# A graph kernel on one core: gather b is issued only when gather b-2 has landed

## What is computed

```python
def _rgcn_conv(x, W, Wroot, b, src, dst, etype):
    xs = x[src]
    seg = dst * R + etype
    sums = segment_sum(xs, seg, N * R)
    cnt = segment_sum(ones, seg, N * R)
    mean = (sums / maximum(cnt, 1.0)[:, None]).reshape(N, R, -1)
    return x @ Wroot + b + einsum('nrd,rde->ne', mean, W)

h = relu(_rgcn_conv(layernorm(x), W1, Wroot1, b1, ...))
x = x + _rgcn_conv(h, W2, Wroot2, b2, ...)
x = x + ffn(layernorm(x))      # top 2 of 8 experts, 256 -> 1024 (gelu) -> 256
```

## Time and profile before

| | us |
|---|---|
| median of 3 runs without the profiler | 2936.58 |
| lowest and highest of them | 2933.07, 2938.32 |
| span of the profiled execution, first to last instruction | 3487.9 |

### The profile page before, as it was taken

One profiled execution on the slowest core, in us unless ns is written; L12 is line 12 of the kernel. 1 busy time (PEld: TensorE's weight loads), 2 busy tenths in 40 slices (PEclk: granted clock), 3 DMA queues, 4 the chain that ended last, 5 costly groups with the idle time before them and its releaser, 6 DMA issues.

```text
span 3487.9 us, 82172 instructions
## 1 busy us (share of the span) xinstructions
PE 2472.0 (71%) x19212; PEld 1832.7 (53%) x19213; DVE 1780.8 (51%) x4984; ACT 1225.2 (35%) x2344; POOL 1862.5 (53%) x1980
## 2 busy tenths in 40 slices
PE   1346787678687786346776587687877428999999
PEld 0113565356365564114564365465656327888887
DVE  7324455345355454124454354354545338787777
ACT  5202343134243342012343143152432126555554
POOL 1666566655655554666556656655563543333333
PEclk9557999589799898557998798798997559999999
DMA  6223323233332232223333333333335234322222
GB/s 216 80 83 112 88 87 91 85 87 89 87 88 87 86 89 64 86 84 97 98 104 97 94 100 99 94 105 95 101 100 163 102 115 132 96 73 71 71 70 59
DMA packets 165489, 333.24 MB, mean 96 GB/s; under 512 B 36078, under 2 KB 102346, under 8 KB 165288
## 3 DMA queue, kind: packets, MB, share of 16 engines
q0 software_dynamic: 91632, 247.48, 24.1%
q1 hardware_dynamic: 39912, 41.03, 4.0%
q10 hardware_dynamic: 33872, 43.92, 3.9%
HBM read 285.39 MB, written 49.07 MB: 96 GB/s over the span
## 4 chain that ended last, share of the span: by engine, by line
PE 44%; issue 22%; DVE 10%; another core or an unknown queue 9%; DVEq 7%; SPq 2%; ACT 2%; DMA 1%; ACTq 0%; POOLq 0%; POOL 0%
PE more_banks L1408 13%; PE sum_banks L1384 9%; PE sum_banks L1385 7%; PE more_banks L1535 4%; PE sum_banks L1535 3%; PE more_banks L1400 3%; PE sum_banks L1545 3%; DVEq L1044 3%; DVEq L1041 2%; DVE sels L1044 2%; DVEq L1027 1%; DVE stage L1079 1%; DVE sels L1036 1%; PE sum_banks L1426 1%
## 5 line engine op out<-in xcount | busy, mean ns | idle before, releaser
L509 POOL DMA_INDIRECT ring<-table,tabs x1584 | 1526.9, 964 | 1046.4 <-SPq L399 670.0
L1384 PE MATMUL sum_banks<-ring,sels 128*128 x2348 | 726.6, 311 | 630.1 <-issue 420.1
L1408 PE MATMUL more_banks<-weights,stage 128*128 128x256 f16 x5292 | 919.1, 290 | 22.0 <-issue 21.4
L1385 PE MATMUL sum_banks<-ring,sels 128*128 x2348 | 732.2, 313 | 41.5 <-issue 38.7
L1384 PEld LDWEIGHTS sum_banks<-ring,sels 128*128 128x128 f16 (+1 forms) x2348 | 242.4, 103 | 928.2 <-issue 896.9
L683 ACT ACTIVATE stage<-sum_banks,inv 128x256 f16<-128x256 f32 x784 | 328.1, 473 | 789.5 <-issue 384.9
L1408 PEld LDWEIGHTS more_banks<-weights,stage 128*128 128x128 f16 x5292 | 531.1, 104 | 135.3 <-issue 37.1
L1036 DVE SCALAR_TENSOR_TENSOR sels<-lane,win_off,tabs 128x256 f16<-128x256 f16 x792 | 349.4, 482 | 422.1 <-remote 181.9
L654 ACT ACTIVATE stage<-more_banks 128x1024 f16<-128x1024 f16 x392 | 402.0, 1026 | 419.1 <-remote 405.6
L1044 DVE TENSOR_SCALAR sels<-lane,win_off,tabs 128x128 f16 x780 | 260.6, 334 | 495.8 <-issue 339.6
L1079 DVE SCALAR_TENSOR_TENSOR stage<-sum_banks,inv,stage 128x256 f16<-128x256 f32 x784 | 347.0, 479 | 57.2 <-issue 40.2
(11 more groups left out here) (319 smaller groups left out, 2407.5 us busy)
## 6 DMA issues: line engine op xcount, KB each, us to landing
ring<-table,tabs POOLq DMA_INDIRECT x1584
weights<-L_ffn_W ACTq DMA_DIRECT2D x96, 178.5 KB
stage<-L_ffn_W ACTq DMA_DIRECT2D x16, 1024.0 KB, 5.0
edge_work<-lot_in SPq DMA_DIRECT2D x54, 260.0 KB
table<-edge_work ACTq DMA_DIRECT2D x49, 128.0 KB
lot_in<-sels SPq DMA_DIRECT2D x8, 260.0 KB
weights<-L_gnn_W SPq DMA_DIRECT2D x2, 1024.0 KB, 8.3
weights<-L_gnn_W ACTq DMA_DIRECT2D x2, 1024.0 KB
```

What stands on the lines that cost most here:

```text
L509: pool.indirect_dma_start(ring_rows[:, b % RING, 0:2 * D], None, tables[layer], bass.IndirectOffsetOnAxis(row_tab[:, b:b + 1], 0)).then_in ...
L1384: pe.matmul(to[:, 0:D + 1], hot, ring_row[:, ds(at + D, D + 1)], start=first, stop=last, skip_group_check=True)
L1385: return pe.matmul(to[:, 0:D], hot, ring_row[:, ds(at, D)], start=False, stop=last, skip_group_check=True)
L1408: return [pe.matmul(ps_out[par], rows[:, xp * KD + k, :], w16[:, wp, k, r * D:(r + 1) * D], start=part == PART_ORDER[0] and n == 0, stop=p ...
```

## The change

POOL gets one more wait before each gather from the third of a layer on: for the semaphore that the DMA of gather b-2 raises, at the value that says that all of it has landed. It is the same condition on which SP's `landed` waits. The slot wait stays, ahead of it.

```diff
     RING = 16
     AHEAD = RING // 2
+    BEHIND = 2
...
                 for b in range(GATHERS):
                     if b >= RING:
                         pool.wait_ge(slots_free[layer], b - RING + 1)
+                    if b >= BEHIND:
+                        s = (b - BEHIND) % RING
+                        pool.wait_ge(gathered[s], (b - BEHIND) // RING * 16 + 16 * (USES[s] * layer + 1))
                     pool.indirect_dma_start(ring_rows[:, b % RING, 0:2 * D], None, tables[layer],
                                             bass.IndirectOffsetOnAxis(row_tab[:, b:b + 1], 0)).then_inc(gathered[b % RING], 16)
```

## The result

| | before | changed |
|---|---|---|
| median us (4 runs each) | 2937.45 | 3744.24 |
| lowest and highest | 2933.07, 2940.33 | 3739.47, 3747.62 |
| profiled span | 3487.9 | 3736.6 |

The ratio is 1.2749, with a 95% interval of 1.2731 to 1.2767: 807 us slower. The direction and the bound were as forecast, the amount was not: it came to twice the 404 us, outside the range.

What follows compares the result with a forecast made beforehand. POOL's gather rate was taken to bound the graph layers: two gathers take 2.78 + 0.26 us, 1.52 us each; 1582 x 1.52 plus 965.9 us outside, less corrections of 20, 4.3 and 6 us, gives 3340 us, range 3120 to 3450 us.

Steps and rivals of the forecast that it cites:

- the 404 us: Whole kernel: the forecast slowdown, 13.7%, to 3340 us; 68% for 3250 to 3430 us.
- The reading of the bound: Graph layers: the profile's extra 551 us are recording pauses; timed, POOL's gather rate is the bound, 1.246 us per interval.
- the 965.9: Time outside the 1582 gather intervals, in us: 84.3 before the first, 850.1 from the last's start, 31.5 between layers.
- The landing: Graph layers: from a gather's start on POOL to its landing, taken as 2.78 us, with 2.9 us the other end.
- The second wait: POOL from the 17th gather on: likely an instruction for one of two waits, costed at nothing, up to 0.1 us a pair.
- 0.26: POOL's wake, in us, from the release of a wait to the gather's start; bounds 0.2 and 0.3 us.
- my corrections: Taken off the sum: 20 us of backlog at layer ends, 4.3 us at the ring's start, 6 us for the count.
- Rival (a), the slack takes it: Graph layers: 670.0 us of slot waits absorb the longer intervals, about 2937 us, no change; 4%.
- Rival (b), a shorter landing: Gathers land sooner than traced: 0.5 us less gives 2945 us (5%), half of that 3135 us (11%).
- Rival (c): Graph layers: fewer gathers in flight leave POOL's issue undisturbed, 24 us won, 2913 us; 1%.
- Rival (d), late landings: Graph layers: long landings no longer absorbed, 1.60 us an interval, 3467 us; 11%.
- L399's waits: POOL's 574 waits for a free ring slot before gathers, 670.0 us in the profile; forecast to fall by more than half.

Runs made afterwards that it cites:

- The second profile of before: The unchanged kernel before, profiled once more with no edit: 2934.0 us in its one timed run, profiled span 2931.9 us.
- the swapped one: The changed kernel with its two waits in the other order, landing of gather b-2 first, then the free slot: 3360.5 us, ratio 1.146.

## Why the prediction failed, step by step

*The reading of the bound held.* That the 551 us were no part of the timed kernel, that it is bound by POOL's gathers, and that the full cost of an interval would show in the time, all rested on an inference. The second profile of before and the run with less TensorE work bear it out. So do four kernels (the changed one, the swapped one and the two with one gather in flight): with intervals from 1.56 to 3.53 us, what lies outside the intervals stays at 892 to 894 us in their traces, so that all of an interval's growth is in the time. The counting was less good: not all of the pauses lay in the layers, 68 us of the 965.9 were pauses too (965.9 - 897.6), and the interval of the timed kernel before was 1.286 us and not 1.246.

*The landing held.* 2.78 us was taken; the changed kernel's chain shows 2.74, 2.76 and, now and then, more. From a gather's start to SP's mark of its landing the median is 2.77 us and the mean 2.88.

*The second wait is the step that failed.* The prediction costed it "at nothing", with "up to 0.1 us a pair" as its end. It was some 0.48 us a pair (0.74 us in place of 0.26). With the order turned round the changed kernel loses 384 of its 807 us, and 384 is nearly all of the 404 us by which the forecast was short. The 20 us that are left between 3360 and the forecast are two smaller errors against each other: an interval of 1.56 and not 1.52 us (63 us more, 20 of them at the 14 gathers above; late landings can explain the rest), and 42 us too much outside the intervals after my corrections (935.9 against some 894).

The reason for the mistake is in how were read. There the semaphore instruction is followed by a gather 0.31 us behind the last, so it looked free. But it had been over before POOL got to it. It said nothing of an instruction whose wait ends last. The same stage of the kernel before has that case too, and I should have taken it for the upper end: VectorE's two rows end at 3101.67 us, and POOL, whose semaphore instruction (L550) waits for them, starts its transfer 0.98 us later.

```profile
3100.80 0.87 DVE L1305 SCALAR_TENSOR_TENSOR edge_work<-edge_work,lot_w 128x256 f32<-128x256 f32 x2
...
3102.65 1.02 POOL L552 DMA_INDIRECT out<-edge_work,lot_ids  x1 [5.92 <-DVE edge_work L1305]
```

With it in place of 0.26 a pair could have taken up to 2.78 + 0.98 = 3.76 us, 1.88 each, and the range would have reached 935.9 + 1582 x 1.88 = 3910 us. The question that I didn't ask was which of the two waits stands on the gather and which ahead of it.

*Rival (a), the slack takes it,* fell with the pauses. *Rival (b), a shorter landing,* too: the landing is the same in profiles without pauses. The fit of the Trainium skill ("DMA: Bandwidth & Descriptors", Anatomy of one DMA, SWDGE path), which gives an estimate of 2.3 us for such a transfer, isn't borne out here; the traces have 2.7 to 2.8 us from POOL's start to the semaphore. *Rival (c)* had no part: POOL's mean is 962 ns. *Rival (d), late landings,* is real and small: in the run with three in flight they cost 34 us.

*What the profile should have shown.* Starts forecast as 1.25 and then 1.8 us apart came 1.25 and 2.25 us apart. That L399's waits would fall by more than half was wrong in name: the profile's rule puts 976 waits down to its successor, L400. The span was foretold as 3600 to 3800 us and is 3736.6, for another reason than the one given, since no gather caught up in pauses.

## What to carry to other kernels

When a wait is added to an instruction that already has one, ask which of them stays on the instruction and which becomes an instruction ahead of it: the one that ends last should be on the instruction itself, here a matter of swapping two lines and 384 us. A limit of n DMAs in flight makes each take (landing + restart)/n, and is free once that is clearly under the issue time; here 2 is far too few, 3 still costs 1.9%, 8 nothing (4 to 7 were not run). And where a profiled span is much longer than the timed runs, find the stretch before believing any wait in it, or take the profile again.

## What was not expected of the hardware

A gather whose own wait ends last starts 0.24 to 0.3 us after its release. Behind a separate semaphore instruction it starts 0.71 to 0.74 us after that has passed. I take the difference, some 0.48 us, for the time in which POOL makes the gather's instruction ready, which would be over already when the wait is on the gather itself; the runs show its size and that it is hidden behind the gather ahead when the wait is over early, and not what happens in it.

With one to three gathers in flight, the same 14 gathers, mostly 98 apart, start some 2 us late in the traces of the order slot then landing (1.3 us or more in the other order), and none do with eight in flight. The cause is open.

One profiled execution was 551 us longer than the timed runs; in it VectorE's bookkeeping instructions took up to 1395 ns (110 ns at most in the second profile), and TensorE and VectorE had gaps of over 3 us that nothing in the profile ended. Eight other profiles, most of kernels with the same instructions on those engines, had spans within 8 us of the timed runs. What sets them off stays open.
